# Two-way decayed scan with a sign-weight product on one core: transposes at the head of a step, sigmoids in threes, stores and halves moved

## The chip, the core and the metric

The kernel runs on 1 core of one Trainium2 chip. The metric is the device time of one execution in microseconds (us). Engines are named as the profile names them: PE (TensorE, the matrix engine), DVE (VectorE), ACT (ScalarE), POOL (GpSimd), SP (SyncE, which here only issues transfers).

## The reference

Inputs are x and k (4 x 1024 x 1024, float32), cond (4 x 256), w and u (1024), weight (1024 x 1024) and bias (1024). k stands for both k and v of the formula, x for r.

```
tf    = sigmoid(sum(cond))                         # one number a batch
decay = exp(-exp(w)) * (0.5 + 0.5 * tf)            # one a channel and batch
ek = exp(min(k, 30)); ekv = ek * k
nf, df = scan(a = a * decay + ekv), scan(b = b * decay + ek)   # along the sequence
nb, db = the same two scans backwards
euk = exp(min(u + k, 30))
num = nf + nb - ekv + euk * k
den = df + db - ek + euk
r   = sigmoid(x) * num / max(den, 1e-8) * (0.8 + 0.2 * tf)
out = x + r @ (sign(weight) * mean|weight|).T + bias
```

## The kernel before

**Tiles and steps.** The work is cut into N = 32 tiles, one for each batch (4) and each block of 128 channels (8). A tile is 128 channels x 1024 points of the sequence, with channels in partitions. `step(n)` of each engine runs once for each tile number n, and engines meet only through semaphores. The order in which an engine does its work is written out by hand in its block, and each engine does its list in that order. A tile goes through three steps: step n does its exponentials and scans, step n+1 its reciprocal and gate, step n+2 its numerator product and the split into two halves for the matrix product.

**What each engine does in step n**, with the names used below:

- DVE: `val` (L929) and `own` (L932) of tile n, both reading kT from PSUM; two scans forward (L901), two backward (L915); then **den** (L953), the denominator of tile n, the one full-size DVE operation of a step both of whose inputs lie in SBUF (euk and terms); then the **gate** of tile n-1 (L944), which multiplies the refined reciprocal in wkv by the turned sigmoid in sT. gate waits for POOL's inv of tile n-1 and for sT of tile n-1. val of tile n+1 follows.
- ACT: **Ln** and **Exp** of tile n-1 (L684, L686), the reciprocal by logarithm, which waits for den of tile n-1; from step 9 on a *clearing* (L663 takes a unit of the product out of PSUM to y_fm, L672 takes the turned unit before it to o_nat); **halves** of tile n-2 (L693, L695), after POOL's base; **two** of tile n-1 (L745), after POOL's chk; the three exponentials of tile n+1 (L649, L652, L653), which need kT; one or two more clearings; in steps 0 to 7 the preparation of a block of the weight (L774, L778, L795); and in some steps a **set** of sigmoids: table load, sigmoids in place on x_nat or x_end (L784, L790), table load back (L785, L791).
- POOL: **base** of tile n-2 (L363, after gate of tile n-2); **chk** of tile n-1 (L375, after Exp); **lo** of tile n-2 (L343, after halves); **inv** of tile n-1 (L381, after chk and two); an accumulating transfer of own (L384, after the third scan of DVE); and the **store** of a finished tile of the output (L356, an accumulating transfer from o_nat to DRAM, which waits until both halves are copied).
- PE: a unit is 16 matmuls of 128x512 (half a tile of the output over all 8 channel blocks). In step n: the first unit of the step, `s_turn(n-1)` (8 transposes of the sigmoid tile into sT), `k_turn(n+1)` (8 transposes of k into kT, after own of tile n), then the other units, each followed by the four transposes of the unit before (yT), which need ACT's clearing. From step 30 on PE makes the last batch's product, in the natural orientation (L484).
- SP: in step n the load of k of tile n+3 (after k_turn(n+1)), the load of x of tile n+2 (after s_turn(n-1), which frees the buffer), and copies of x into the output for the stores to add to.

`made(n)`, `cleared(n)` and `added` fix how many units are made and cleared by step n and in which step a tile is stored: two units a step in steps 9 to 18, two or three up to 24, three or more from 25. Tile m is stored in `summed(n)`: one a step in steps 11 to 27 and in 31, two in steps 28, 29 and 30. o_nat has four buffers, so the first copy of tile m waits until the store of tile m-4 has landed.

The sigmoid sets are made in even steps up to 24 (tiles n and n+1) and in steps 11, 13 and 15 (two each of the last six tiles, which lie in x_end).

Of the kernel before, what the change touches and what calls it, by code (L numbers as in the profile page):

```python
# [42 lines left out]
def bi_wkv_binary_ffn(nc, x, k, cond, w, u, weight, bias, out):  # L43
# [47 lines left out]
    with ExitStack() as ctx:  # L91
# [56 lines left out]
        two = sb("two", [P, 1])  # L148
# [104 lines left out]
        def _(sp):  # L253
# [28 lines left out]
            def step(n, p, wt, nxt, nxt3, mid, low, late):  # L282
                if wt:

                    done(sp, "sgn", n - 2)
                    done(sp, "abs", n - 2)
                    sp.dma_start(w_nat[p][:, :], weight.rearrange("(o p) i -> o p i", p=P)[n])\
                      .then_inc(w_in[p], 16)
                if n == 0:
                    load_x(2)  # L290
                if nxt3:

                    done(sp, "kT", n + 1)
                    sp.dma_start(k_nat[1 - p][:, :, :], tile_of(k, n + 3)).then_inc(k_in[1 - p], 16)
                if mid and n + 2 < SOON:

                    done(sp, "sT", n - 1)
                    load_x(n + 2)
                if 4 <= n < 10:
                    sp.dma_start(x_of(SOON + n - 4), tile_of(x, SOON + n - 4)).then_inc(s_soon, 16)  # L300
                if n == N - 2:

                    done(sp, "sT", N - 4)
                    load_tail(5)
                    done(sp, "kT", N - 2)
                    load_tail(6)
                if n == N - 1:

                    done(sp, "sT", N - 3)
                    load_tail(7)  # L310
                if 1 <= n <= 3 * TT:
                    fill((n - 1) // TT, (n - 1) % TT)
                if 1 <= n <= TT:
                    fill_last(n - 1)
# [18 lines left out]
        def _(pool):  # L333
# [31 lines left out]
            def step(n, p, wt, nxt, nxt3, mid, low, late):  # L365
                W, R = wkv[1 - p][:, :], rec[1 - p][:, :]
                if low:
                    base(n - 2)
                if 3 <= n < TT + 3:
                    biases(n - 3)  # L370
# [16 lines left out]
                for m in summed(n):  # L387
                    store(m)
# [23 lines left out]
        def _(pe):  # L412
# [90 lines left out]
            def step(n, p, wt, nxt, nxt3, mid, low, late):  # L503
# [30 lines left out]
                split = units[0:3 if n == LAST + 1 else 2] if first else ()  # L534
                if first and n != LAST + 1:
# [4 lines left out]
                if mid and not sooner:  # L540
                    s_turn(n - 1)
# [4 lines left out]
                if nxt:  # L546
                    k_turn(n + 1, 1 - p)
                if ahead:
# [82 lines left out]
        def _(act):  # L631
# [70 lines left out]
            act.wait_ge(s_const, 5)  # L702
# [12 lines left out]
            def step(n, p, wt, nxt, nxt3, mid, low, late):  # L715
# [6 lines left out]
                if n == N - 1:  # L722
                    early_out(4)
                    early_out(5)
                sooner = cleared(n - 1) if n == LAST + 2 else min(made(n - 1), cleared(n - 1) + 1)
# [10 lines left out]
                if late and n < N - 2:  # L736
                    clear(cleared(n - 1), sooner)
                if low:
# [3 lines left out]
                if mid:  # L742

                    done(act, "chk", n - 1)
                    act.activation(wkv[1 - p][:, :], wkv[1 - p][:, :], ACT.Identity,  # L745
                                   scale=-HI_SCALE * LO_GAIN, bias=two[:, 0:1]).then_inc(st["two"], 1)
# [33 lines left out]
                if p == 0 and n < SOON:  # L780

                    for i in range(2):
                        x_landed(act, n + i)
                        act.activation(x_of(n + i), x_of(n + i), ACT.Sigmoid).then_inc(st["sig"], 1)  # L784
                    act.preload_act_table_set("natural_log_exp_and_others")  # L785
                if n in (11, 13, 15):

                    for i in range(n - 11, n - 9):
                        act.wait_ge(s_soon, 16 * (N - SOON))
                        act.activation(x_of(SOON + i), x_of(SOON + i), ACT.Sigmoid).then_inc(st["soon"], 1)  # L790
# [49 lines left out]
        def _(dve):  # L840
# [15 lines left out]
            dve.memset(two[:, :], 2.0 * HI_SCALE * LO_GAIN).then_inc(s_const, 1)  # L856
# [197 lines left out]
```

## Time and profile before

| | |
|---|---|
| median of 3 runs (lowest, highest) | 529.12 us (527.07, 530.0) |
| the profiled execution: time, span | 530.84 us, 528.9 us |
| mean granted PE clock | 0.866 of full |
| busy, share of the span | PE 67%, DVE 93%, ACT 82%, POOL 72% |
| steps 1 to 30, start of den(0) to start of den(30) | 20.8 us to 471.2 us |
| from start of den(30) to the end of the span | 57.7 us |

The profiled execution's time is 1.9 us more than its span and 1.7 us above the median. In step n the stretch from one den to the next is what one tile costs. Below, den(n) is den of tile n, made in step n, and so for the others.

### The profile page before, as it was taken

How to read it: one execution, taken by the hardware profiler on the slowest of the kernel's cores; microseconds unless marked ns; L12 is line 12 of the kernel's file. 1: busy time of each engine (PE TensorE's matmuls, PEld its weight loads, DVE VectorE, ACT ScalarE, POOL GpSimd, SP SyncE). 2: the span in 40 equal slices, each digit the busy share in tenths (PEclk: the TensorE clock that was granted, in tenths of full speed). 3: DMA queues.
4: the chain of work that ended last, by engine and by line, in shares of the span. 5: the costliest groups of instructions: out<-in, count | busy, mean ns of one | idle time of the engine just before them, and what ended most of it. 6: DMA issues, size and time to landing. Idle time of an engine off the chain costs nothing.

```text
span 528.9 us, 5414 instructions
## 1 busy us (share of the span) xinstructions
PE 353.6 (67%) x1803; PEld 203.9 (39%) x1803; DVE 494.5 (93%) x347; ACT 431.8 (82%) x473; POOL 381.9 (72%) x210
## 2 busy tenths in 40 slices
PE   3332132333298775876768698878759995989996
PEld 2221122233054333443434354544425553544442
DVE  6999999999999999999999999899999999598676
ACT  3979899899989999999999979899698884884500
POOL 0058677858786877777788876969688776979483
PEclk9996565566698989898899998996979997999999
DMA  8677899999988778986879779597656569678469
GB/s 228 170 239 238 257 230 267 255 287 243 271 215 198 171 176 172 198 175 105 192 170 215 171 151 216 82 253 143 135 105 119 93 107 119 140 128 118 54 99 221
DMA packets 101283, 94.22 MB, mean 178 GB/s; under 512 B 2924, under 2 KB 93064, under 8 KB 100744
## 3 DMA queue, kind: packets, MB, share of 16 engines
q0 software_dynamic: 31440, 36.18, 45.1%
q1 hardware_dynamic: 67720, 56.65, 34.3%
q10 hardware_dynamic: 2096, 1.05, 0.7%
q8 instruction: 15, 0.25, 0.2%
q14 instruction: 12, 0.10, 0.1%
HBM read 60.31 MB, written 37.75 MB: 185 GB/s over the span
## 4 chain that ended last, share of the span: by engine, by line
ACT 42%; PE 26%; issue 12%; POOL 10%; DMA 5%; DVE 4%; SPq 0%; ACTq 0%; DVEq 0%; POOLq 0%
PE prod L443 11%; DMA out_dram<-o_nat 5%; ACT euk L653 5%; ACT rec L684 4%; POOL wkv L375 4%; POOL acts L343 4%; ACT x_nat L784 4%; ACT terms L649 3%; ACT y_fm L663 3%; PE prod L484 3%; ACT L785 3%; ACT L784 3%; ACT acts L693 2%; ACT o_nat L672 2%; ACT rec L695 2%
## 5 line engine op out<-in xcount | busy, mean ns | idle before, releaser
L443 PE MATMUL prod<-acts,sgn 128*128 128x512 f16 x752 | 189.2, 409 | 13.3 <-ACT orow L800 10.9
L915 DVE TENSOR_TENSOR_SCAN terms<-cols,y_start,terms 128x1024 f32<-128x1024 f32 x64 | 147.0, 2337 | 1.3 <-DVE y_start L907 0.2
L901 DVE TENSOR_TENSOR_SCAN terms<-cols,terms 128x1024 f32<-128x1024 f32 x64 | 142.7, 2269 | 0.0
L375 POOL TENSOR_TENSOR wkv<-euk,rec 128x1024 f32<-128x1024 f32 x31 | 76.3, 2462 | 62.2 <-ACT rec L686 62.2
L443 PEld LDWEIGHTS prod<-acts,sgn 128*128 128x128 f16 x752 | 78.1, 104 | 106.4 <-issue 24.9
L363 POOL TENSOR_TENSOR wkv<-wkv,terms 128x1024 f32<-128x1024 f32 x31 | 81.3, 2623 | 25.0 <-DVE wkv L944 24.9
L343 POOL TENSOR_TENSOR acts<-wkv,rec 128x1024 f16<-128x1024 f32 x30 | 71.2, 2375 | 22.5 <-ACT rec L695 22.5
L381 POOL TENSOR_TENSOR wkv<-wkv,rec 128x1024 f32<-128x1024 f32 x31 | 74.3, 2396 | 1.3 <-ACT wkv L745 1.3
L418 PE MATMUL yT<-ident,y_fm 128*128 128x128 f32 x192 | 31.5, 289 | 55.6 <-ACT o_nat L672 55.1
L953 DVE SCALAR_TENSOR_TENSOR euk<-euk,terms 128x1024 f32<-128x1024 f32 x31 | 63.8, 2058 | 1.1
L418 PE MATMUL prod<-ident,o_nat 128*128 128x128 f16 x64 | 8.3, 310 | 72.7 <-ACT o_nat L778 72.7
L418 PEld LDWEIGHTS yT<-ident,y_fm 128*128 128x128 f32 x192 | 22.7, 147 | 68.5 <-ACT y_fm L663 58.5
L944 DVE SCALAR_TENSOR_TENSOR wkv<-wkv,sT 128x1024 f32<-128x1024 f32 x31 | 37.5, 1211 | 8.7 <-POOL wkv L381 8.7
L356 POOL DMA_DIRECT2D out_dram<-o_nat x24 | 44.5, 1980 | 0.0
L649 ACT ACTIVATE terms<-kT,cap 128x1024 f32<-128x1024 f32 x31 | 34.2, 1102 | 11.4 <-PE kT L418 11.4
L418 PE MATMUL kT<-ident,k_nat 128*128 128x128 f32 x248 | 38.8, 309 | 6.4 <-DVE own L932 6.3
L663 ACT ACTIVATE y_fm<-prod,bcol,oscale 128x512 f32<-128x512 f32 x47 | 36.2, 771 | 6.7 <-PE prod L443 4.5
L672 ACT COPY o_nat<-yT 128x512 f32<-128x512 f32 x48 | 27.8, 580 | 16.7 <-DMA out_dram<-o_nat 11.4
L745 ACT ACTIVATE wkv<-wkv,two 128x1024 f32<-128x1024 f32 x31 | 35.3, 1140 | 7.3 <-POOL wkv L375 7.3
L384 POOL DMA_DIRECT2D terms<-own x32 | 28.8, 901 | 17.1 <-DVE terms L915 17.1
L929 DVE TENSOR_TENSOR terms<-terms,kT 128x1024 f32<-128x1024 f32 x32 | 38.7, 1211 | 2.2 <-ACT euk L653 2.2
L418 PE MATMUL sT<-ident,x_nat 128*128 128x128 f32 x208 | 35.2, 325 | 8.2 <-ACT x_nat L784 7.3
(122 smaller groups left out, 606.9 us busy)
## 6 DMA issues: line engine op xcount, KB each, us to landing
terms<-own POOLq DMA_DIRECT2D x32, 512.0 KB, 5.3
out_dram<-in_x_dram SPq DMA_DIRECT2D x32, 512.0 KB, 6.5
k_nat<-in_fside_BxSxS_dram SPq DMA_DIRECT2D x30, 512.0 KB, 3.9
x_nat<-in_x_dram SPq DMA_DIRECT2D x26, 512.0 KB, 5.9
out_dram<-o_nat POOLq DMA_DIRECT2D x24, 512.0 KB, 8.1
y_fm<-in_L_ffn_weight_dram SPq DMA_DIRECT2D x8, 512.0 KB, 7.3
out_dram<-in_L_ffn_bias_dram POOLq DMA_DIRECT2D x8, 512.0 KB, 6.7
x_end<-in_x_dram SPq DMA_DIRECT2D x6, 512.0 KB, 8.8
```

The lines of the kernel that those rows point to most:

```text
L343: pool.tensor_tensor(acts[:, 1, n % (2 * CT), :], wkv[p][:, :], rec[p][:, :], ALU.subtract)\
L356: pool.dma_start(tile_of(out, m), o_nat[m % NO][:, :, :], accum_op=ALU.add)\
L363: pool.tensor_tensor(wkv[n % 2][:, :], wkv[n % 2][:, :], ekv[n % NV], ALU.mult).then_inc(st["base"], 1)
L375: pool.tensor_tensor(W, euk[1 - p][:, :], R, ALU.mult).then_inc(st["chk"], 1)
L381: pool.tensor_tensor(W, W, R, ALU.mult).then_inc(st["inv"], 1)
L418: ins = pe.transpose(dst(q), what(q), one)
L443: ins = pe.matmul(made_in(u), view[:, c, m % CT * P:m % CT * P + P], acts[:, part, m // CT % 2 * CT + c, h * H:(h + 1) * H], start=(part = ...
L649: act.activation(ek[p], kT[:, :], ACT.Relu, scale=-1.0, bias=cap[:, 0:1]).then_inc(st["below"], 1)
L663: act.activation(y_fm[m % 2][:, h * H:(h + 1) * H], made_in(u), ACT.Identity, scale=oscale[:, m:m + 1], bias=bcol[:, m:m + 1]).then_inc(st ...
L901: dve.tensor_tensor_scan(buf, d, buf, 0.0, ALU.mult, ALU.add).then_inc(st["F" + kind], 1)
L915: dve.tensor_tensor_scan(buf[:, ::-1], d, buf[:, ::-1], y_start[:, i:i + 1], ALU.mult, ALU.add)\
L953: dve.scalar_tensor_tensor(U, U, E30, E, ALU.min, ALU.add).then_inc(st["den"], 1)
```

## The change

Six edits, all of order but the last two:

- **PE** in steps up to 25: s_turn and k_turn stand at the head of a step, ahead of its first unit. In steps 26 to 29 s_turn stood there already and k_turn stays behind the first unit.
- **SP**: the load of x stands ahead of the load of k.
- **ACT, sigmoids**: sets are made in steps 0, 3, 6, ... 24, each of tiles n, n+1 and n+2 (n+2 is loaded in the same step); from step 9 on each takes one tile of the last six with it. So there are 9 sets in place of 16, with 32 sigmoids as before. From step 9 to 21 a set has four sigmoids, before two.
- **ACT, halves**: in steps 4, 7, 10, ... 22 (those behind a set; a clearing stands there only from step 10 on) halves and two stand ahead of the first clearing, which comes behind two.
- **POOL**: the first store of a step stands behind base and ahead of chk, except in step 31; before, it stood at the end of the step. The second store of steps 28 to 30 stays at the end.
- **ACT, two**: the operation is Copy with a constant bias, before Identity with a bias from a tile; the tile `two` and its memset on DVE are gone, and a semaphore count goes from 5 to 4.

```diff
@@ SP, step
+                if mid and n + 2 < SOON:
+                    done(sp, "sT", n - 1)
+                    load_x(n + 2)
                 if nxt3:
                     done(sp, "kT", n + 1)
                     sp.dma_start(k_nat[1 - p][:, :, :], tile_of(k, n + 3)).then_inc(k_in[1 - p], 16)
-                if mid and n + 2 < SOON:
-                    done(sp, "sT", n - 1)
-                    load_x(n + 2)
@@ POOL, step
+                ready = summed(n)
                 if low:
                     base(n - 2)
+                if n < N - 1:
+                    for m in ready[0:1]:
+                        store(m)
+                    ready = ready[1:]
...
-                for m in summed(n):
+                for m in ready:
                     store(m)
@@ PE, step
+                if mid and not sooner:
+                    s_turn(n - 1)
+                    k_turn(n + 1, 1 - p)
+                if n == 0:
+                    k_turn(n + 1, 1 - p)
                 if first and n != LAST + 1:
                     done(pe, "ev", units[0] - 2)
                     part(units[0], 0, CT - 1)
                 elif units and not first:
                     unit(units[0])
-                if mid and not sooner:
-                    s_turn(n - 1)
+                if sooner:
+                    k_turn(n + 1, 1 - p)
                 if ahead:
                     turned(made(n) - 1)
                     for u in (made(n) + 1, made(n) + 2):
                         part(u, 0, CT - 2)
-                if nxt:
-                    k_turn(n + 1, 1 - p)
-                if ahead:
@@ ACT, step
+                hasty = low and n < LAST and n % 3 == 1
+                if hasty:
+                    done(act, "base", n - 2)
+                    halves(n - 2, p)
...
-                if late and n < N - 2:
+                if late and n < N - 2 and not hasty:
                     clear(cleared(n - 1), sooner)
-                if low:
+                if low and not hasty:
                     done(act, "base", n - 2)
                     halves(n - 2, p)
                 if mid:
                     done(act, "chk", n - 1)
-                    act.activation(wkv[1 - p][:, :], wkv[1 - p][:, :], ACT.Identity,
-                                   scale=-HI_SCALE * LO_GAIN, bias=two[:, 0:1]).then_inc(st["two"], 1)
+                    act.activation(wkv[1 - p][:, :], wkv[1 - p][:, :], ACT.Copy,
+                                   scale=-HI_SCALE * LO_GAIN, bias=2.0 * HI_SCALE * LO_GAIN).then_inc(st["two"], 1)
+                if late and hasty:
+                    clear(cleared(n - 1), sooner)
...
-                if p == 0 and n < SOON:
-                    for i in range(2):
-                        x_landed(act, n + i)
-                        act.activation(x_of(n + i), x_of(n + i), ACT.Sigmoid).then_inc(st["sig"], 1)
-                    act.preload_act_table_set("natural_log_exp_and_others")
-                if n in (11, 13, 15):
-                    for i in range(n - 11, n - 9):
+                if n % 3 == 0 and n < SOON:
+                    for i in range(n, min(n + 3, SOON)):
+                        x_landed(act, i)
+                        act.activation(x_of(i), x_of(i), ACT.Sigmoid).then_inc(st["sig"], 1)
+                    if n >= 9:
                         act.wait_ge(s_soon, 16 * (N - SOON))
-                        act.activation(x_of(SOON + i), x_of(SOON + i), ACT.Sigmoid).then_inc(st["soon"], 1)
+                        i = SOON + n // 3 - 3
+                        act.activation(x_of(i), x_of(i), ACT.Sigmoid).then_inc(st["soon"], 1)
                     act.preload_act_table_set("natural_log_exp_and_others")
```

POOL, from inv of step 11 to base of step 12, before (the third row is the transfer of own, the fourth the store):

```order
L381 TENSOR_TENSOR wkv0<-wkv0,rec0 128x1024
L384 DMA terms<-own1 128x1024
L356 DMA out_0_dram<-o_nat0 128x8x128
L363 TENSOR_TENSOR wkv0<-wkv0,terms 128x1024
L375 TENSOR_TENSOR wkv1<-euk1,rec1 128x1024
```

POOL, from base to base of step 11 after the change:

```order
L362 TENSOR_TENSOR wkv1<-wkv1,terms 128x1024
L355 DMA out_0_dram<-o_nat0 128x8x128
L379 TENSOR_TENSOR wkv0<-euk0,rec0 128x1024
L342 TENSOR_TENSOR acts<-wkv1,rec1 128x1024
L385 TENSOR_TENSOR wkv0<-wkv0,rec0 128x1024
L388 DMA terms<-own1 128x1024
```

The store of the first output tile has gone from behind own's transfer to between base and chk.

ACT, from the end of step 12 to the exponentials of step 13, before (set of two, then Ln, Exp, clearing, halves, two):

```order
L784 ACT_TABLE_LOAD
L784 ACTIVATE x_nat2<-x_nat2 128x1024
L784 ACTIVATE x_nat0<-x_nat0 128x1024
L785 ACT_TABLE_LOAD
L684 ACTIVATE rec0<-euk0,lnb 128x1024
L686 ACTIVATE rec0<-rec0 128x1024
L663 ACTIVATE y_fm1<-prod,bcol,oscale 128x512
L672 COPY o_nat1<-yT 128x512
L693 ACTIVATE acts<-wkv1 128x1024
L695 ACTIVATE rec1<-acts 128x1024
L745 ACTIVATE wkv0<-wkv0,two 128x1024
L649 ACTIVATE terms<-kT,cap 128x1024
```

ACT behind a later set, from the end of step 15 into step 16, after the change:

```order
L796 ACT_TABLE_LOAD
L796 ACTIVATE x_nat0<-x_nat0 128x1024
L796 ACTIVATE x_nat1<-x_nat1 128x1024
L796 ACTIVATE x_nat2<-x_nat2 128x1024
L801 ACTIVATE x_end<-x_end 128x1024
L802 ACT_TABLE_LOAD
L690 ACTIVATE rec1<-euk1,lnb 128x1024
L692 ACTIVATE rec1<-rec1 128x1024
L699 ACTIVATE acts<-wkv0 128x1024
L701 ACTIVATE rec0<-acts 128x1024
L755 ACTIVATE wkv1<-wkv1 128x1024
L669 ACTIVATE y_fm0<-prod,bcol,oscale 128x512
```

The set has grown by two sigmoids, and the clearing (L663, now L669) has gone behind two (L745, now L755).

PE in one step of two units, before and then after the change (sT is s_turn, kT is k_turn, prod a unit, yT the turning of a cleared unit):

```order
L443 MATMUL prod<-acts,sgn 128x512 x16
L418 MATMUL sT<-ident,x_nat2 128x128 x8
L418 MATMUL kT<-ident,k_nat0 128x128 x8
L418 MATMUL yT<-ident,y_fm1 128x128 x4
L443 MATMUL prod<-acts,sgn 128x512 x16
L418 MATMUL yT<-ident,y_fm0 128x128 x4
```

```order
L422 MATMUL sT<-ident,x_nat2 128x128 x8
L422 MATMUL kT<-ident,k_nat0 128x128 x8
L447 MATMUL prod<-acts,sgn 128x512 x16
L422 MATMUL yT<-ident,y_fm1 128x128 x4
L447 MATMUL prod<-acts,sgn 128x512 x16
L422 MATMUL yT<-ident,y_fm0 128x128 x4
```

The two turns have passed the first unit.

## Rows read from the trace of the kernel before

**Rows 1.** Timeline of DVE: start, us, operation (den in three steps).

```profile
107.14 1.22 DVE L953 SCALAR_TENSOR_TENSOR euk<-euk,terms 128x1024 f32<-128x1024 f32 x1
...
224.46 2.80 DVE L953 SCALAR_TENSOR_TENSOR euk<-euk,terms 128x1024 f32<-128x1024 f32 x1
...
239.96 2.79 DVE L953 SCALAR_TENSOR_TENSOR euk<-euk,terms 128x1024 f32<-128x1024 f32 x1
```

**Rows 2.** den alone (L953) by stage: length, busy us (times), PE clock, DMA, GB/s.

```profile
20.00:167.00 147.00, 19.88 (x11) 0.69 0.92 244
167.00:275.00 108.00, 18.65 (x7) 0.93 0.78 167
275.00:377.50 102.50, 11.54 (x7) 0.92 0.81 166
377.50:474.00 96.50, 13.74 (x6) 0.91 0.69 122
```

**Rows 3.** Timeline of POOL, in brackets idle before: step 15, then later steps.

```profile
228.48 2.52 POOL L363 TENSOR_TENSOR wkv<-wkv,terms 128x1024 f32<-128x1024 f32 x1
...
236.99 2.37 POOL L343 TENSOR_TENSOR acts<-wkv,rec 128x1024 f16<-128x1024 f32 x1 [0.83 <-ACT rec L695]
239.31 2.36 POOL L381 TENSOR_TENSOR wkv<-wkv,rec 128x1024 f32<-128x1024 f32 x1
...
242.19 1.92 POOL L356 DMA_DIRECT2D out_dram<-o_nat  x1
...
329.67 3.33 POOL L381 TENSOR_TENSOR wkv<-wkv,rec 128x1024 f32<-128x1024 f32 x1
...
437.27 3.52 POOL L356 DMA_DIRECT2D out_dram<-o_nat  x2
...
489.78 1.59 POOL L356 DMA_DIRECT2D out_dram<-o_nat  x1
```

**Rows 4.** DVE's waits, all of the span: total us, times, longest us.

```profile
DVE wkv L944 <- POOL wkv L381: 8.7, 3, 4.6
...
DVE terms L929 <- ACT euk L653: 2.2, 2, 2.0
```

**Rows 5.** Timeline of ACT: step 15 and the set behind it.

```profile
231.49 1.15 ACT L684 ACTIVATE rec<-euk,lnb 128x1024 f32<-128x1024 f32 x1
...
236.82 1.14 ACT L745 ACTIVATE wkv<-wkv,two 128x1024 f32<-128x1024 f32 x1
...
242.64 1.28 ACT L790 ACT_TABLE_LOAD   x1
243.93 2.00 ACT L790 ACTIVATE x_end<-x_end 128x1024 f32<-128x1024 f32 x2
...
247.25 1.15 ACT L684 ACTIVATE rec<-euk,lnb 128x1024 f32<-128x1024 f32 x1
```

**Rows 6.** Timeline of ACT: Ln in steps 2, 3 and 4.

```profile
37.45 1.14 ACT L684 ACTIVATE rec<-euk,lnb 128x1024 f32<-128x1024 f32 x1
...
54.16 1.14 ACT L684 ACTIVATE rec<-euk,lnb 128x1024 f32<-128x1024 f32 x1
...
67.37 1.14 ACT L684 ACTIVATE rec<-euk,lnb 128x1024 f32<-128x1024 f32 x1
```

**Rows 7.** Timeline of ACT in steps 24, 25 and 28: waits for kT and for a store.

```profile
374.82 1.11 ACT L649 ACTIVATE terms<-kT,cap 128x1024 f32<-128x1024 f32 x1 [4.04 <-PE kT L418]
...
382.80 1.15 ACT L684 ACTIVATE rec<-euk,lnb 128x1024 f32<-128x1024 f32 x1
...
445.54 0.59 ACT L672 COPY o_nat<-yT 128x512 f32<-128x512 f32 x1 [7.46 <-DMA out_dram<-o_nat]
```

**Rows 8.** PE behind that wait; then one stretch, busy us of PE, PEld, DVE, ACT, POOL.

```profile
446.26 1.08 PE L418 MATMUL yT<-ident,y_fm 128*128 128x128 f32 x4 [6.58 <-ACT o_nat L672]
...
448.85 5.28 PE L443 MATMUL prod<-acts,sgn 128*128 128x512 f16 x16
...
480.00:503.00 23.00, 23.00 (x112) 10.89 (x110) 16.80 (x19) 10.89 (x17) 15.03 (x10) 1.00 0.54 74
```

More of the change, by code:

```diff
@@ L147, in bi_wkv_binary_ffn @@
         lnb = sb("lnb", [P, 1])
-        two = sb("two", [P, 1])
         tiny = sb("tiny", [P, 1])
@@ L700, in early_out @@
                 act.copy(park[i], park_bank[i]).then_inc(st["early_sb"], 1)
-            act.wait_ge(s_const, 5)
+            act.wait_ge(s_const, 4)
             act.wait_ge(s_ucol, 2)
@@ L855, in _ @@
             dve.memset(lnb[:, :], LN_BIAS).then_inc(s_const, 1)
-            dve.memset(two[:, :], 2.0 * HI_SCALE * LO_GAIN).then_inc(s_const, 1)
             dve.memset(tiny[:, :], TINY).then_inc(s_const, 1)
```

## The prediction

> **What bounds the kernel now.** I read the busy shares first: DVE is busy for 93% of the span, and from step 1 to step 30 almost without a gap. But den is not the same length each time. It takes 1.22 us in one step and 2.80 in another, with the same shape [rows 1]. By stages its 31 runs sum to 19.88, 18.65, 11.54 and 13.74 us [rows 2]; less 1.22 for each that is 6.5, 10.1, 3.0 and 6.4 us, 26.0 in all, that den spends standing. The timelines of DVE and POOL laid side by side say for what. den(15) starts at 239.96 while inv runs from 239.31 to 241.67, and ends at 242.75, one den later than inv [rows 1, 3]. So a step has a wait inside a busy instruction: den, with both inputs in SBUF, stands while POOL computes. It goes the other way too: an inv that came while den ran, at 329.67, took 3.33 in place of 2.36 [rows 3], and gate waited for it instead. gate needs inv in any case, so the measure is how much later inv ends than den could start. Real idle time adds 4.6 (gate, step 29), 2.2 (gate, step 21), and 2.2 at val, mostly in step 29 [rows 4]; the last 1.9 of gate's 8.7 lie behind den(30). The four stages thus lose 6.5, 10.1, 5.5 and 13.0 us, 35.1 in all, against steps of 13.92 us. That is the step without loss: den to den 15.50 less (2.80 - 1.22) [rows 1].
>
> **The ring that makes inv late.** Let Z be the end of den(n-1), here 227.26. den(n) can start at Z + 12.70 (239.96). Ln starts at Z + 4.23, since ACT is still in a set, and inv ends at 241.67, that is 10.18 after Ln; 0.83 of it is POOL waiting for halves, which stand behind a clearing [rows 3, 5]. With halves ahead it is 9.35. So Ln may start up to Z + 2.5, or Z + 3.3 with halves ahead, and each us beyond costs one. In steps 10 to 16 ACT makes a set in every step, and it goes without a gap from Ln to Ln in 15.76 (231.49 to 247.25), so ACT sets the pace there, not DVE.
>
> **Sets by three.** A set of two costs 4.61 (242.64 to 247.25), of which the sigmoids are 2.00 and the two table loads with their ends 2.6 [rows 5]. Sixteen sets become nine: 7 x 2.6 = 18 us less on ACT, of which only what makes inv early counts. The other side is that a set of four takes 4.61 + 2.0 = 6.6 at a stretch.
>
> A price to weigh here: the first sigmoid stands 1.29 behind the start of the table load (242.64 to 243.93 [rows 5]), so a load brings no pause with it. The Trainium skill (ScalarE: Activation LUTs, What ACT_TABLE_LOAD costs) gives about 2.66 us a switch, a drain of 1.38 included. By the page a set of two would be 7.3 us and the cut 37 us; the row disagrees, and I go by the row.
>
> **Stores ahead of chk.** This lengthens POOL's own chain in every step that stores, 11 to 30. base starts at Z + 1.22 and POOL goes from one operation to the next in 2.32 (236.99 to 239.31). A store costs POOL 1.59 right behind an operation and 1.92 behind a transfer [rows 3]. So chk starts at Z + 5.1 to 5.4, not at Z + 3.5, and inv ends at best at Z + 12.1 to 12.4. That is inside 12.70, with 0.3 to 0.6 to spare: cost nothing on DVE. But two then starts at Z + 7.5 to 7.8, and ACT has 5.8 left behind it (236.82 to 242.64 [rows 5]): it ends at Z + 13.3 to 13.6, in time for the next Ln. In a set step it ends at Z + 20.1, so Ln starts at Z' + 6.0 to 6.2 (Z' = Z + 13.92), and inv ends 2.7 late, with halves ahead. The two steps that follow carry nothing over. The cost is 2.7 in three steps where it was about 1.6 in each.
>
> **The sum by stage.**
> - Up to den(10): no stores. ACT takes 13.2 for a step without a set (54.16 to 67.37) and 16.7 with one of two (37.45 to 54.16) [rows 6], so 17.7 with three: 44.1 for three steps against 41.8 of DVE. Worked forward from 38.5 in step 2, Ln of step 4 stands at 69.4, 6.5 behind den(3), which costs 3.1; that of step 7 costs 2.4; steps 2 and 10 some 0.2 each. 5.9 for 6.5.
> - 11 to 17: 2 x 2.7 = 5.4 for 10.1.
> - 18 to 24: step 19 costs 2.7; step 20, where the third unit is late as now, 0.3; step 22 follows a set with one more clearing behind it (1.1 more), 3.8. kT at the head takes away the wait of 4.04 in step 24 [rows 7] and with it the 0.3 at val. 6.8 for 5.5.
> - 25 to 30: without the wait of 4.04 for kT, Ln of step 25 starts 2 us earlier against DVE, though its set has three: from Z + 5.8 (382.80) to Z + 3.7, leaving 0.4 for 2.0. The store of tile 17 is issued at Z + 3.6 of step 28, near 426, not at 437.27; with 8.2 to land it is there at 434, before the copy that now waits 7.46 until 445.54 [rows 3, 7]. So the idle 4.6 and 2.0 and the long dens of 28 to 30 go. Three units a step still leave waits for PE: 0.5 to 1 a step. 3.0 for 13.0.
>
> 21.1 for 35.1: 14.0 us less. The profiled execution took 530.84, which gives 516.8; it stands 1.7 above the median, so 515.0.
>
> **What lies beside other work.** The turns at the head: PE waits for own of tile n until Z + 3.5 with a unit behind it, which before ran in that time. A unit is then made by Z + 8.1, and its clearing stands behind expU at Z + 12: hidden while there are two units. If that cover goes (three units, or a unit that takes 5.28 as at 448.85 [rows 8]), the last unit slips into the next step, up to 1 us a step. k's load behind x's: both wait for turns that are now earlier. The x tile of the same step is issued near Z + 2.5 and wanted, as third sigmoid, near Z + 16. With the 8.2 that the store of 437.27 took to land, the nearest row, it is there at Z + 10.7. two as Copy and a memset less: a few hundredths of a us on ACT, nothing on the path.
>
> **Does the tail keep it?** From 480 to 503 PE is busy for all of 23.00 us, DVE for 16.80 [rows 8], so the end is PE's. PE gains too: it was idle for 6.58 ahead of 446.26, and the 16 matmuls behind took 5.28, where 112 in 23.00 us make 3.3 for 16 [rows 8], 2.0 more. Together 8.6, and its last batch starts with lo(23), 2 us earlier against DVE. That is about what DVE gains in the last stage (10.0), so I take off nothing.
>
> **Rivals.**
> - *The late gain is not kept.* PE or the clearings behind it bound steps 26 to 31 in their own right, and PE's new idle time is spent again at the end. Then about half of the 10.0 is left: 518 to 523, say 520. For it: PE is full from 480. Against: its two stretches above. 16%.
> - *Sets cost little.* If ACT loses no time to chk in a set step, its load is what counts: 15.76 less 4.61 is 11.15 a step, with a set of four 40.1 in three steps, under the 41.8 of DVE. Then the 21.1 that is left shrinks to about 11, and the time is 505. Against: POOL's order holds two back until chk is through. 13%.
> - *POOL's chain is too long (slower).* The slack is 0.3 to 0.6 us. Two stores in a row took 3.52, 1.8 each [rows 3]. If a store between two operations holds POOL for 3.0, chk starts at Z + 6.5, inv ends at Z + 13.5 and each of 20 steps pays 0.8: 16 us, which takes the gain: 531. At 3.5 it is 541. It decides from about 2.9 us a store. Against: 1.59 in the one row of a store behind an operation. 8%.
> - *It does not do what it says:* x tiles of a set arrive late since their buffer comes free only in the same step. The margin is 5 us; if loads took 15, each of 8 sets would wait 1 to 2: 525. 4%.
>
> **Numbers.** Forecast 515.0 (510 to 520), 59%. With 16% for 518 to 523, 13% for about 505, 12% for 525 and more, the range is 505 to 524. One measurement of this kernel can tell about 0.5%, 2.6 us, from no change. Faster by more than that (below 526.5) 83%; within it 8%; slower 9%.
>
> **What would show it.** Right: den at 1.22 in all steps but those with n = 1 mod 3, where it is 3 to 4 or gate idles; two at Z + 7.5 behind a store; Ln right behind den in steps 12, 14, 15, 17; no wait of ACT for a store in steps 28 and 29; 19 table loads; PE full from about 465. Wrong: den long in every step with a store (third rival); ACT waiting for x or PE for sigmoids; den(30) early but the end not.

## The result, and the profile after

The changed kernel takes 514.12 us, median of four runs (513.96 to 514.45); the kernel before, beside it, 528.79 (527.07 to 530.0). The ratio is 0.9726, with a 95% interval of 0.9697 to 0.9754. The profiled execution took 513.96, with a span of 512.1 at a mean granted clock of 0.862. In what follows one run, of e8, took 757.95 us and stays out of that kernel's time and ratio.

The first lines of the page of after: span, busy shares, and the groups that answer to den, two, the store and gate (busy us, mean ns | idle us before, releaser).

```profile
span 512.1 us, 5399 instructions
...
PE 354.7 (69%) x1803; PEld 209.6 (41%) x1803; DVE 482.4 (94%) x346; ACT 411.1 (80%) x459; POOL 381.1 (74%) x210
...
L963 DVE SCALAR_TENSOR_TENSOR euk<-euk,terms 128x1024 f32<-128x1024 f32 x31 | 52.8, 1704 | 1.1
L755 ACT ACTIVATE wkv<-wkv 128x1024 f32<-128x1024 f32 x31 | 32.7, 1055 | 23.6 <-POOL wkv L379 23.6
...
L954 DVE SCALAR_TENSOR_TENSOR wkv<-wkv,sT 128x1024 f32<-128x1024 f32 x31 | 37.6, 1212 | 4.6 <-POOL wkv L385 4.6
...
L355 POOL DMA_DIRECT2D out_dram<-o_nat x24 | 39.9, 1662 | 0.0
```

DVE is the bound as before, and den still stands: 52.8 us in 31 runs, where 31 x 1.22 would be 37.8. By [rows 2] it was 63.8. A store holds POOL for 1.66 on average. den by stage, the same four stages as [rows 2]; columns length, busy us (times), PE clock, DMA share, GB/s:

```profile
20.00:177.00 157.00, 17.78 (x11) 0.70 0.92 242
177.00:278.00 101.00, 12.71 (x7) 0.92 0.85 178
278.00:381.00 103.00, 14.09 (x7) 0.90 0.76 165
381.00:460.00 79.00, 8.24 (x6) 0.96 0.81 136
```

Less 1.22 for each run this is 4.4, 4.2, 5.6 and 0.9 us (before 6.5, 10.1, 3.0 and 6.4). With the idle time of DVE in each step added (gate 4.6 in all, in steps 4 and 22; before 8.7) I get what each stage loses against 13.92 us a step. The same count, made step by step up to the end of den(30), for every kernel of this study (the prediction had before at 35.1 by its own count; waits behind den(30) are not in it, and two counts of the same stage can differ by 0.2):

| kernel | to den(10) | 11 to 17 | 18 to 24 | 25 to 30 | sum |
|---|---|---|---|---|---|
| before | 6.6 | 10.2 | 5.7 | 13.1 | 35.6 |
| forecast for after | 5.9 | 5.4 | 6.8 | 3.0 | 21.1 |
| after | 6.9 | 4.2 | 7.9 | 0.9 | 19.9 |
| e1: stores alone | 6.6 | 10.1 | 5.1 | 0.0 | 21.9 |
| e2: after, stores at the end | 7.2 | 1.9 | 5.8 | 8.9 | 23.8 |
| e3: after, stores ahead only late | 7.0 | 1.8 | 5.7 | 1.5 | 16.1 |
| e4: after, clearing first | 8.5 | 6.0 | 8.0 | 1.6 | 24.1 |
| e5: after, PE as before | 6.4 | 4.2 | 7.0 | 3.4 | 21.0 |
| e6: sets alone | 7.7 | 2.9 | 4.1 | 13.1 | 27.9 |
| e7: after, den with PSUM operand | 4.9 | 2.2 | 3.8 | 2.9 | 13.9 |
| e8: e3, clearing first in step 19 | 7.9 | 1.7 | 4.0 | 1.3 | 14.8 |
| e9: after, bias transfer last | 7.4 | 4.2 | 7.0 | 1.4 | 20.1 |
| e10: e3, bias transfer last | 7.8 | 1.6 | 3.7 | 1.4 | 14.5 |

**A step with a set and the step behind it.** DVE first: Z is the end of the den at 179.45, so 180.67; den(12) starts at 193.37, den(13) at 207.29.

```profile
179.45 1.23 DVE L963 SCALAR_TENSOR_TENSOR euk<-euk,terms 128x1024 f32<-128x1024 f32 x1
...
193.37 1.23 DVE L963 SCALAR_TENSOR_TENSOR euk<-euk,terms 128x1024 f32<-128x1024 f32 x1
...
207.29 3.28 DVE L963 SCALAR_TENSOR_TENSOR euk<-euk,terms 128x1024 f32<-128x1024 f32 x1
```

POOL in the same two steps: the store between base (L362) and chk (L379), then lo (L342) and inv (L385).

```profile
181.90 2.36 POOL L362 TENSOR_TENSOR wkv<-wkv,terms 128x1024 f32<-128x1024 f32 x1 [2.13 <-DVE wkv L954]
184.22 1.59 POOL L355 DMA_DIRECT2D out_dram<-o_nat  x1
185.19 2.99 POOL L379 TENSOR_TENSOR wkv<-euk,rec 128x1024 f32<-128x1024 f32 x1
187.51 3.00 POOL L342 TENSOR_TENSOR acts<-wkv,rec 128x1024 f16<-128x1024 f32 x1
189.83 2.98 POOL L385 TENSOR_TENSOR wkv<-wkv,rec 128x1024 f32<-128x1024 f32 x1
...
202.51 2.35 POOL L379 TENSOR_TENSOR wkv<-euk,rec 128x1024 f32<-128x1024 f32 x1 [2.78 <-ACT rec L692]
...
207.14 2.34 POOL L385 TENSOR_TENSOR wkv<-wkv,rec 128x1024 f32<-128x1024 f32 x1
```

ACT: Ln (L690), two (L755), then the set of four and the next Ln.

```profile
180.71 1.15 ACT L690 ACTIVATE rec<-euk,lnb 128x1024 f32<-128x1024 f32 x1 [0.95 <-DVE euk L963]
...
188.22 1.06 ACT L755 ACTIVATE wkv<-wkv 128x1024 f32<-128x1024 f32 x1 [1.78 <-POOL wkv L379]
...
193.68 1.28 ACT L796 ACT_TABLE_LOAD   x1
194.97 2.95 ACT L796 ACTIVATE x_nat<-x_nat 128x1024 f32<-128x1024 f32 x3
197.83 1.04 ACT L801 ACTIVATE x_end<-x_end 128x1024 f32<-128x1024 f32 x1
198.89 1.28 ACT L802 ACT_TABLE_LOAD   x1
200.19 1.15 ACT L690 ACTIVATE rec<-euk,lnb 128x1024 f32<-128x1024 f32 x1
```

Step 12 shows the slack of the prediction: inv ends at 192.81, Z + 12.1, and den, which can start at Z + 12.7, is 1.23 long. In step 13 Ln starts at 200.19, 5.6 behind den(12); inv runs from 207.14 to 209.48, den comes at 207.29 into it and stands: 3.28.

**The late steps.** Here [rows 7] had a wait of 7.46 for a store. In after ACT has no wait for a store at all, and losses are 0.0 in steps 28 to 30. From 463 to 486 PE has no gap (length; PE, PEld, DVE, ACT, POOL; clock, DMA share, GB/s), as [rows 8] had from 480:

```profile
463.00:486.00 23.00, 23.00 (x113) 10.94 (x111) 17.33 (x20) 10.26 (x16) 15.06 (x10) 1.00 0.36 52
```

### The profile page after: what moved, and what is told of

It reads as the page before. It is cut to its first block, busy times and chain, and to the rows that moved or that the text cites. A ratio compares the mean times of both kernels' runs of the same rounds, so it can differ in the third digit from the quotient of the medians.

```text
span 512.1 us, 5399 instructions
## 1 busy us (share of the span) xinstructions
PE 354.7 (69%) x1803; PEld 209.6 (41%) x1803; DVE 482.4 (94%) x346; ACT 411.1 (80%) x459; POOL 381.1 (74%) x210
## 3 DMA queue, kind: packets, MB, share of 16 engines
q1 hardware_dynamic: 67720, 56.65, 35.1%
q10 hardware_dynamic: 2096, 1.05, 0.8%
## 4 chain that ended last, share of the span: by engine, by line
POOL 23%; ACT 23%; PE 22%; issue 16%; DVE 14%; DMA 0%; SPq 0%; DVEq 0%; ACTq 0%; POOLq 0%
POOL wkv L379 9%; PE prod L447 8%; DVE terms L925 4%; POOL acts L342 4%; DVE terms L911 4%; POOL wkv L385 4%; POOL out_dram L355 3%; PE prod L488 3%; ACT x_nat L796 3%; ACT rec L690 2%; ACT terms L655 2%; ACT euk L659 2%; ACT rec L692 2%; PE sT L488 2%; PE kT L488 2%
## 5 line engine op out<-in xcount | busy, mean ns | idle before, releaser
L447 PE MATMUL prod<-acts,sgn 128*128 128x512 f16 x752 | 180.2, 395 | 0.0
L362 POOL TENSOR_TENSOR wkv<-wkv,terms 128x1024 f32<-128x1024 f32 x31 | 73.4, 2367 | 50.7 <-DVE wkv L954 50.7
L379 POOL TENSOR_TENSOR wkv<-euk,rec 128x1024 f32<-128x1024 f32 x31 | 82.3, 2654 | 37.2 <-ACT rec L692 37.2
L385 POOL TENSOR_TENSOR wkv<-wkv,rec 128x1024 f32<-128x1024 f32 x31 | 81.8, 2639 | 1.2 <-ACT wkv L755 1.2
L342 POOL TENSOR_TENSOR acts<-wkv,rec 128x1024 f16<-128x1024 f32 x30 | 77.7, 2590 | 4.7 <-ACT rec L701 4.6
L422 PE MATMUL kT<-ident,k_nat 128*128 128x128 f32 x248 | 45.9, 347 | 16.7 <-DVE own L942 16.5
L963 DVE SCALAR_TENSOR_TENSOR euk<-euk,terms 128x1024 f32<-128x1024 f32 x31 | 52.8, 1704 | 1.1
L755 ACT ACTIVATE wkv<-wkv 128x1024 f32<-128x1024 f32 x31 | 32.7, 1055 | 23.6 <-POOL wkv L379 23.6
L388 POOL DMA_DIRECT2D terms<-own x32 | 35.8, 1120 | 17.4 <-DVE terms L925 17.2
L422 PEld LDWEIGHTS kT<-ident,k_nat 128*128 128x128 f32 x248 | 38.7, 184 | 23.7 <-issue 22.7
L422 PEld LDWEIGHTS sT<-ident,x_nat 128*128 128x128 f32 x208 | 31.3, 179 | 28.8 <-issue 16.3
L669 ACT ACTIVATE y_fm<-prod,bcol,oscale 128x512 f32<-128x512 f32 x47 | 36.1, 769 | 4.8 <-PE prod L447 2.7
L422 PEld LDWEIGHTS yT<-ident,y_fm 128*128 128x128 f32 x192 | 23.8, 148 | 38.9 <-ACT y_fm L669 32.7
L690 ACT ACTIVATE rec<-euk,lnb 128x1024 f32<-128x1024 f32 x31 | 35.7, 1151 | 4.5 <-DVE euk L963 4.4
```

Of the source, the lines that this page charges most:

```text
L342: pool.tensor_tensor(acts[:, 1, n % (2 * CT), :], wkv[p][:, :], rec[p][:, :], ALU.subtract)\
L362: pool.tensor_tensor(wkv[n % 2][:, :], wkv[n % 2][:, :], ekv[n % NV], ALU.mult).then_inc(st["base"], 1)
L379: pool.tensor_tensor(W, euk[1 - p][:, :], R, ALU.mult).then_inc(st["chk"], 1)
L385: pool.tensor_tensor(W, W, R, ALU.mult).then_inc(st["inv"], 1)
L422: ins = pe.transpose(dst(q), what(q), one)
L447: ins = pe.matmul(made_in(u), view[:, c, m % CT * P:m % CT * P + P], acts[:, part, m // CT % 2 * CT + c, h * H:(h + 1) * H], start=(part = ...
```

## The experiments

Times are medians; ratios are to the kernel before, run on the same chip, with 95% intervals. The load of x ahead of the load of k, and two as a Copy (1.06 us in place of 1.14), were not tried alone.

**e1, stores alone.** Before, with the first store of a step behind base:

```diff
+                ready = summed(n)
                 if low:
                     base(n - 2)
+                if n < N - 1:
+                    for m in ready[0:1]:
+                        store(m)
+                    ready = ready[1:]
...
-                for m in summed(n):
+                for m in ready:
```

> The kernel before with one edit: the first store of a step ahead of chk. Theory (near the end the store frees o_nat in time; elsewhere it costs only where rec comes before Z + 5): in steps 12 to 17 rec comes at Z + 6.5 and nothing changes; the losses of steps 28 to 30 (1.8, 6.7 and 1.5 us) and nearly 1 us of the tail go; behind the sets of steps 18 to 24 some 3 us are added: about 520.5 us. Rival (the late gain of the change comes from PE's new order): the waits for a store go but the end stays, 526 to 529 us.

518.43 us, 0.9786 (0.9754 to 0.9818), so 11.3 less. The last stage goes from 13.1 to 0.0, though PE's order is that of before. Steps 27 to 30 had 11.1 of it, and there the store frees o_nat in time. The other 2.0, in step 25, went in another way: ACT's wait for kT in step 24 fell from 4.04 to 0.15 (by all steps from 11.4 to 7.8), and PE ran at another clock. PE in step 24, before and then e1:

```profile
364.27 1.94 PE L418 MATMUL sT<-ident,x_nat 128*128 128x128 f32 x8 [0.90 <-DVE wkv L944]
366.85 7.05 PE L443 MATMUL prod<-acts,sgn 128*128 128x512 f16 x24
```

```profile
363.92 1.06 PE L423 MATMUL sT<-ident,x_nat 128*128 128x128 f32 x8 [0.90 <-DVE wkv L949]
365.26 5.34 PE L448 MATMUL prod<-acts,sgn 128*128 128x512 f16 x24
```

From 364 to 370 the granted clock was 0.50 in before and 1.00 in e1. No run shows that the store did this, so these 2.0 us are not shown to be the stores'. Steps 18 to 24 change little: 0.6 less at step 20, 0.9 less at 21, 1.1 more at 19. The time is 2 us below the 520.5 expected. Steps 10 to 17 are unchanged to 0.1: a store ahead of chk costs nothing there even with a set in every step. That speaks against the third rival, which wanted 0.8 a step.

**e6, sets alone.** Before, with the set block of after:

```diff
-                if p == 0 and n < SOON:
+                if n % 3 == 0 and n < SOON:
...
-                    for i in range(2):
+                    for i in range(n, min(n + 3, SOON)):
...
-                if n in (11, 13, 15):
+                    if n >= 9:
```

> The kernel before with one edit: sigmoids in sets of three (from step 9 four). Theory (in steps 11 to 17 ACT sets the pace, 15.5 us a step, and is freed): the loss of 10.1 us there falls to about 4, up to step 10 it grows by 1, from 18 to 24 it stays, near the end it stays: about 522.5 us. Rival (the sets alone change only when ACT waits, and the gain needs halves ahead of the clearing): 527 us or more.

524.23 us, 0.9896 (0.9856 to 0.9931), 5.5 less. Steps 11 to 17 lose 2.9 in place of 10.2, the last stage its 13.1 as before. This is 1.7 above the 522.5 expected. e1 and e6 together would give 16.8; after, with further edits, gives 14.5: stores and sets get in each other's way, and e3 shows where.

**e2, stores back at the end of the step**, else as after:

```diff
-                if n < N - 1:
-                    for m in ready[0:1]:
-                        store(m)
-                    ready = ready[1:]
```

> The changed kernel with every store back at the end of its step. Theory (a store ahead of chk costs 1.6 us on POOL, holds two back to Z + 7.5 and so lengthens what is left of a set step, but frees o_nat in time near the end): behind sets two no longer waits, the loss in steps 13, 16 and 19 falls from 2.05 us to about 1.0 and in step 22 from 3.2 to about 2.2, together 4 us less; the waits of ACT for a store in steps 28 to 30 come back, 8 to 9 us more. Sum 514.1 + 4.5 = about 518.5 us. Rival (the loss behind a set does not depend on the store): 2.05 stays in steps 13, 16, 19, and the time is about 522.5 us.

519.36 us, 0.9827 (0.9784 to 0.9869), near the 518.5 expected. The last stage loses 8.9 (after 0.9), gate stands idle for 2.25 more behind den(30), and the wait of [rows 7] is back in the timeline of ACT (in brackets the idle time ahead of the copy into o_nat):

```profile
436.17 0.58 ACT L674 COPY o_nat<-yT 128x512 f32<-128x512 f32 x1 [7.50 <-DMA out_dram<-o_nat]
```

But steps 11 to 17 lose only 1.9, and 18 to 24 only 5.8. Stores at the head pay late and cost early.

**e3, stores at the head only from step 25 on:**

```diff
-                if n < N - 1:
+                if LAST < n < N - 1:
```

> The changed kernel with stores at the head only in steps 25 to 30, at the end up to step 24. Theory: takes both gains, losses behind sets of 1.0 in steps 13, 16, 19 and about 2.2 in step 22, no wait for a store near the end: 514.1 - 4 = about 510 us, faster than the changed kernel. Rival: the store's place up to step 24 has no weight, 514 us.

509.17 us, 0.9638 (0.9598 to 0.9679): faster than both kernels, as expected, and 4.7 less than after by the ratios, whose intervals don't meet. From e2 it differs only in the stores from step 25 on, and these are worth 10.2 us. Step 12 and 13 of POOL: inv and own's transfer first, then the store; and den(13) behind it.

```profile
188.92 2.36 POOL L385 TENSOR_TENSOR wkv<-wkv,rec 128x1024 f32<-128x1024 f32 x1
191.47 0.90 POOL L388 DMA_DIRECT2D terms<-own  x1 [0.19 <-issue]
192.07 1.92 POOL L355 DMA_DIRECT2D out_dram<-o_nat  x1
```

```profile
207.36 2.53 DVE L963 SCALAR_TENSOR_TENSOR euk<-euk,terms 128x1024 f32<-128x1024 f32 x1
```

den(13) stands for 1.3 in place of 2.06, den(16) for 0.5 in place of 2.08, and step 22 loses 1.8 in place of 3.2. In a set step ACT's list waits for two, two for chk, and chk for the store; in the steps without a set, ACT has time to spare.

**e4, the clearing ahead of halves in every step:**

```diff
-                hasty = low and n < LAST and n % 3 == 1
+                hasty = False
```

> The changed kernel with the first clearing ahead of halves in every step, as before the change. Theory (lo waits for halves, so inv ends 0.8 us later behind each set): losses in steps 10, 13, 16, 19 and 22 grow by 0.8 each, the others stay: about 518 us. Rival (ACT's debt behind a set is what counts, and the place of the clearing within the step is free): 514 us, and lo starts right behind chk in these steps all the same.

518.06 us, 0.9814 (0.9775 to 0.9853), 4.7 more than after: the time expected, but by other terms. Steps 10, 13, 16, 19 and 22 lose 1.7, 0.9, 0.9, 0.9 and 0.9 more. But step 20 goes from 1.64 to 0.0, more than halves ahead bring in step 19. In after, the clearing behind two in step 19 comes late, the third unit with it. ACT up to the halves of step 20:

```profile
300.75 0.78 ACT L669 ACTIVATE y_fm<-prod,bcol,oscale 128x512 f32<-128x512 f32 x1 [1.60 <-issue]
...
304.64 0.78 ACT L669 ACTIVATE y_fm<-prod,bcol,oscale 128x512 f32<-128x512 f32 x1 [0.50 <-PE prod L447]
...
305.78 1.07 ACT L699 ACTIVATE acts<-wkv 128x1024 f16<-128x1024 f32 x1
```

ACT stands 1.6 ahead of the last clearing of step 19 and 0.5 ahead of the first of step 20; halves follow at 305.78, and lo on POOL, which waits 1.42 for them, makes inv late. The 1.6 end when PE's unit does. It took 5.30, at a mean granted clock of 0.68, behind 3.10 us in which PE waited for the late clearing. In e10 (below), which has the same order here, PE stood for 1.41 and the unit took 3.62, at full clock. PE in step 19, after and then e10:

```profile
294.89 0.63 PE L422 MATMUL yT<-ident,y_fm 128*128 128x128 f32 x4 [3.10 <-ACT o_nat L678]
295.36 5.30 PE L447 MATMUL prod<-acts,sgn 128*128 128x512 f16 x16
```

```profile
291.65 0.63 PE L422 MATMUL yT<-ident,y_fm 128*128 128x128 f32 x4 [1.41 <-ACT o_nat L678]
292.11 3.62 PE L447 MATMUL prod<-acts,sgn 128*128 128x512 f16 x16
```

Step 20 lost 1.64 in after and 0.45 in e10.

**e8, e3 with the clearing ahead of halves in step 19 alone:**

```diff
-                hasty = low and n < LAST and n % 3 == 1
+                hasty = low and n < LAST and n % 3 == 1 and n != 19
```

> The changed kernel with stores at the head only in steps 25 to 30, and in step 19 the clearing ahead of halves again. Theory (in step 19, the first with three units, a clearing behind two delays PE's third unit into step 20): step 19 loses 0.9 us more, step 20 loses 1.6 less, so 0.7 us less than with stores at the head only in steps 25 to 30, about 508.5 us. Rival (step 20 loses for another reason): 510 us.

508.76 us, 0.9622 (0.9581 to 0.9662). Step 20 loses 0.0, and step 19 the same 1.35, not 0.9 more as expected. So the place of the clearing is shown as a cause of step 20's loss; how much it costs hangs on PE's clock behind it, as e10 shows with 0.45. The time can't be told from e3's: step 10 lost 0.9 more, step 13 0.8 less and step 16 0.7 more, where nothing was changed. Step 9 on PE explains the first of these. In after: sT and kT turns, then the two units of the step.

```profile
138.58 1.94 PE L422 MATMUL sT<-ident,x_nat 128*128 128x128 f32 x8 [8.25 <-DVE wkv L954]
140.84 1.65 PE L422 MATMUL kT<-ident,k_nat 128*128 128x128 f32 x8 [0.32 <-DVE own L942]
142.33 7.07 PE L447 MATMUL prod<-acts,sgn 128*128 128x512 f16 x32
```

And in e8:

```profile
138.58 1.94 PE L422 MATMUL sT<-ident,x_nat 128*128 128x128 f32 x8 [8.24 <-DVE wkv L954]
140.84 1.94 PE L422 MATMUL kT<-ident,k_nat 128*128 128x128 f32 x8 [0.32 <-DVE own L942]
142.57 7.90 PE L447 MATMUL prod<-acts,sgn 128*128 128x512 f16 x32
```

PE idles 8.25 ahead of the turns, and from 136 to 142 the granted clock is 0.50 (1.2 GHz). From 142 to 150 it is 1.00 in after, 0.86 in e8: the same 32 matmuls take 7.07 and 7.90. The clearing of step 9 and the set of four behind it start 1.1 later, and step 10 loses 2.7 in place of 1.6, most of it with gate idle.

**e9, the bias transfer of steps 3 to 10 behind own's transfer,** not between base and chk, else as after:

```diff
-                if 3 <= n < TT + 3:
-                    biases(n - 3)
...
                 pool.dma_start(ekv[n % NV], own[p][:, :], accum_op=ALU.add).then_inc(num_in[p], 16)
+                if 3 <= n < TT + 3:
+                    biases(n - 3)
```

> The changed kernel with the transfer of the bias (steps 3 to 10) issued behind own's transfer at the end of POOL's step, not between base and chk. It asks where the 1.62 us that den(10) loses in the changed kernel comes from. There chk of step 9 starts 2.89 behind base, where 2.32 is usual, and two waits 1.05 for it, ahead of a set of four. Theory (POOL's chain in step 9): two of step 9 comes 0.58 earlier, the set and Ln of step 10 with it, less what the clearings then wait for PE (they wait 0.37 now, 0.9 then at most): the loss of step 10 goes from 1.62 to 1.05 to 1.3, all other steps as they are, time 513.7 (513 to 514.5). Rival (the clearings wait for the unit of PE in any case, so the set starts no earlier): step 10 stays at 1.6, time 514.1. The time can't tell them apart; the set's start behind den(8) in the timeline does.

515.32 us, 0.9736 (0.9703 to 0.9769), above the 513 to 514.5 expected and not to be told from after. two of step 9 comes earlier, at 142.96 in place of 144.12 (0.3 of it because all of DVE stands 0.3 earlier here), but step 10 loses 2.33. ACT in step 9:

```profile
142.96 1.06 ACT L755 ACTIVATE wkv<-wkv 128x1024 f32<-128x1024 f32 x1 [0.17 <-POOL wkv L377]
...
149.44 0.78 ACT L669 ACTIVATE y_fm<-prod,bcol,oscale 128x512 f32<-128x512 f32 x1 [1.90 <-PE prod L447]
```

What POOL gave, ACT waits for PE: the rival's mechanism holds, though not its 1.6 for step 10. With the turns at the head the two units of this step start only at 142.3, and here they took 7.47, at a granted clock of 0.93 from 142 to 150. So the set starts at 150.24, later than in after (149.86), and with den(8) 0.3 earlier.

**e10, both:** e3 with that move.

> The changed kernel with stores at the head only from step 25 on, and the bias transfer behind own's transfer. Expected as the kernel with late stores alone (509.2), less 0.3 to 0.6 for step 10: 508.8. It is the fastest list of edits so far, if step 10 gives anything; rival: step 10 unchanged and 509.2.

508.53 us, 0.9609 (0.9572 to 0.9646), within the interval of e3; step 10 lost 2.7, as in e8, at a granted clock of 0.87 from 142 to 150, so no gain from the move is shown. In both kernels step 13 then lost only 0.5: steps 10 and 13 together lost 3.15 in each, and 3.06 in e3.

**e5, PE's order of before,** else as after:

```diff
-                if mid and not sooner:
-                    s_turn(n - 1)
-                    k_turn(n + 1, 1 - p)
...
                     unit(units[0])
+                if mid and not sooner:
+                    s_turn(n - 1)
+                if nxt:
+                    k_turn(n + 1, 1 - p)
```

> The changed kernel with PE's order of before (unit, s_turn, k_turn, then the others), all else as changed. Theory (the turns at the head matter in step 24, where kT comes 4 us sooner, and cost where there are three units): step 25 loses about 2 us more, steps 20 and 24 up to 2 us less, x tiles of a set land in time: 514 to 516 us. Rival (the sets by three need the turns at the head, since the buffer of the third tile comes free only behind s_turn): ACT waits for x in steps 12 to 21, 1 to 3 us each: 519 us or more.

516.44 us, 0.9753 (0.9725 to 0.9781), 1.4 more than after by the ratios and not quite told apart; ACT waits for no x tile, so the rival is out. In the trace step 10 loses 0.5 less, step 24 0.9 less, steps 25 and 27 1.4 and 1.0 more, and step 20 the same: 1.1 in sum. Step 24 is the place where the head order hurts. In after PE turns yT of the unit before only behind kT, and both at the low clock (0.50 from 362 to 365); ACT waits for it:

```profile
362.32 1.94 PE L422 MATMUL kT<-ident,k_nat 128*128 128x128 f32 x8 [0.73 <-DVE own L942]
364.06 1.06 PE L422 MATMUL yT<-ident,y_fm 128*128 128x128 f32 x4
```

```profile
365.15 0.59 ACT L678 COPY o_nat<-yT 128x512 f32<-128x512 f32 x1 [3.69 <-PE yT L422]
```

**e7, den with one input in PSUM.** It asks whether den's length is standing:

```diff
+                    if mid:
+                        done(dve, "sT", n - 1)
-                    dve.scalar_tensor_tensor(U, U, E30, E, ALU.min, ALU.add)
+                    dve.scalar_tensor_tensor(U, U, E30, sT[:, :] if mid else E, ALU.min, ALU.add)
```

> The changed kernel in which den takes its second operand from sT in PSUM and not from ek in SBUF (in steps 1 to 30): the same size, the sums of the denominator are left out. Theory (den stands while POOL reads SBUF, and gate then comes one den later than inv ends): den takes 1.22 us in every step, gate waits idle for inv instead, and each of the steps 4, 7, 10, 13, 16, 19, 20, 22 and 24 loses about 1.0 us less: about 505.5 us. Rival (den is long for a reason of its own, or the wait for inv sets all of the loss): den stays long, or the loss stays the same with gate idle for all of it: 514 us.

509.02 us, 0.9636 (0.96 to 0.9673), 4.8 less than after. The kernel leaves the sums of the denominator out, so that only its time says something. den in this kernel (ns least, median, most), the den and gate of step 7, and the sum of DVE's waits for inv:

```profile
L965 DVE SCALAR_TENSOR_TENSOR euk<-euk,sT x30: 1220/1221/1223, 33.5 to 451.0; 128x1024 f32<-128x1024 f32 x30
```

```profile
118.89 1.22 DVE L965 SCALAR_TENSOR_TENSOR euk<-euk,sT 128x1024 f32<-128x1024 f32 x1
122.08 1.22 DVE L954 SCALAR_TENSOR_TENSOR wkv<-wkv,sT 128x1024 f32<-128x1024 f32 x1 [1.97 <-POOL wkv L385]
```

```profile
DVE wkv L954 <- POOL wkv L385: 11.1, 11, 2.2
```

All 30 are 1.22 long, also where POOL computes: the excess of [rows 1, 2] is standing, for its second input in SBUF. What remains is gate's open wait for inv, 11.1 us where after shows 4.6. In step 13 den's loss of 2.06 has become a wait of 1.03: a den that stands waits for inv's end and then takes its own 1.22 behind it, where one that doesn't stand runs beside inv. The time came out 3.5 above the 505.5 expected, for two reasons in the trace. Step 7 kept 2.05: from two of step 6 on ACT has no pause until Ln, which starts at 112.77 where after has 113.03. And steps 26 and 27 lose 1.17 and 1.46, where after loses 0.0 and 0.50. What holds these two I haven't settled. Step 20 lost 1.2 less, but that is not den's: PE stood for 1.61 in step 19 and its unit took 3.62, as in e10.

The Trainium skill (SBUF — State Buffer, Who interferes with whom) says that a DVE instruction with two SBUF inputs contends with a GpSimd instruction that reads SBUF, one with at most one SBUF input, outside the two-port modes, doesn't, and that the order of issue decides who blocks. The runs agree: up to 3.42 against 1.22 for den, and inv at 3.33 where it came second (before, at 329.67).

## Why the prediction was right

**Stores ahead of chk: right to 0.1 us.** Forecast in a step without a set: two at Z + 7.5 to 7.8, inv's end at Z + 12.1 to 12.4, den at Z + 12.70. Measured: 188.22, 192.81 and 193.37, so Z + 7.5, 12.1 and 12.7. In 11 to 17 only steps 13 and 16 lose anything, as said.

**The loss behind a set: right in kind, too large.** 2.7 was forecast, 2.06, 2.08 and 2.07 were measured (steps 13, 16, 19). Ln stands at Z' + 5.6, not 6.0 to 6.2: the set of four took 6.51 (193.68 to 200.19), and the list from two to the set 5.46, where [rows 5] had 5.82. Steps 4, 7 and 22 were 2.82, 2.20 and 3.24 for 3.1, 2.4 and 3.8. Over the six steps this is 2.9 less than forecast.

**Step 10: 1.62 for 0.2.** The working went by ACT's load alone. In step 9 of after, halves wait 1.34 and two 1.05 for POOL, and the sum had neither; no run takes these waits away alone. It also left out that with the turns at its head PE starts the first two units only at 142.3, behind own of step 9, and that the clearing ahead of the set needs them (e9). The turns are the smaller part: with PE's order of before (e5) the two waits for POOL are the same and step 10 still loses 1.13. Behind 8.25 us of idle PE the granted clock from 142 to 150 differed, and with it the loss: 1.6 at 1.00 (after), 2.7 at 0.86 (e8).

**Step 20: 1.64 for 0.3.** I took the third unit to be late "as now" and didn't follow the clearing of step 19, which had just moved behind two. e4 and e8, each with that clearing ahead, show 0.0. In e10 and e7, which have it behind as after has, the loss is 0.45 and 0.46: there PE idled less and its unit took 3.62, not 5.30. So about 1.2 of the 1.64 came with the lower granted clock, which the sum didn't reckon with.

**Step 24: 0.92 for 0.** The wait of [rows 7] for kT is gone, as forecast, and the one for yT took its place: 3.69 us for 4.04. The turn at the head passed one unit and one yT, and only the unit was counted.

**The last stage: 0.9 for 3.0.** The wait of 7.46 and the long dens of 28 to 30 went, as said. The 0.5 to 1 a step set aside for PE was too much: ACT waits for PE there 0.7 at most, and only steps 25 and 27 lose, 0.4 and 0.5. That kT at the head has a part in this gain, as I wrote, e5 bears out: without it ACT waits 1.74 for kT in step 24, step 25 loses 1.4 more and step 27 1.0. e1, which has 0.0 with PE's order of before, had PE at the full clock in step 24.

**The sum.** Terms too large by 2.9 + 2.1 and too small by 1.4 + 1.3 + 0.9 nearly cancel: 19.9 for 21.1. The start of den(30) moved from 471.2 to 456.8. Behind it the span shrank by 2.5 more, of which 1.5 is den(30) itself, counted in the sum; 1.0 is beyond it. The profiled executions differ by 16.9 us, where 14.0 were forecast; the medians by 14.7, as that of before stood 2.1 above the median of the runs beside the new kernel, and that of after 0.2 below its own. The forecast took off 1.7. The mechanism held where most of the gain was forecast, but that the median came within 0.9 of 515.0 is in part luck: terms of the sum that cancel, and a profiled run of before that stood higher above its median than was taken off.

**The rivals.** The late gain was kept, 12.2 of 13.1. "Sets cost little" did not hold in after; e3, with the store out of the set steps, brings the 19.9 down to 16.1, but its 509.2 is still 4 us above the rival's 505. "POOL's chain is too long" fell by the 1.59 of each store behind base and by e1. x tiles are never waited for by the set: their load lands in 3.6 us (median), margin kept.

## What to carry to other kernels

A piece of work that is moved costs only in those steps where the engine behind it has no time to spare, so ask for each step by itself: here the store at the head is worth 10 us from step 25 on (e2 against e3) and costs 5 in the fourteen steps before (after against e3). e3 takes the gain and leaves the cost. Where an instruction with two SBUF inputs is longer than its fellows, read its length as a wait and look at what POOL does then. When work is put at the head of a list, count everything that it passes (units and yT), not only the one it was meant to pass. And before a loss in one step is put down to an edit, compare the granted clock of that step in both traces.

## What the runs showed of the hardware that I had not expected

- Behind a store three POOL operations are recorded as 2.99, 3.00 and 2.98 us, but start 2.32 apart (185.19, 187.51, 189.83), as those of 2.35 do: the records overlap by 0.67, and the work isn't slower. Their ends can be trusted: chk's is at 188.18, and two, which waits for it, starts at 188.22. So it is the starts that are recorded early. From the end of base (184.26) to the end of chk is 3.92, so the store costs 1.60, its own recorded length. The Trainium skill (Perfetto Trace Analysis, GPSIMD Engine Instruction) calls the recorded span of such instructions unreliable and advises to time them from start to start. For the three operations the trace agrees; for the store it doesn't, as from base's start to chk's there are 3.29, only 0.97 more than 2.32.
- The granted clock of a stretch behind an idle one differs between executions of the same instructions: 1.00, 0.98 (e3) and 0.86 (e8) from 142 to 150, with all that is ahead of it alike. It moved the loss of step 10 by 0.9 to 1.1 us, between kernels that don't differ up to there. Between e3 and e8 step 13 gave nearly all of it back. How much of the spread between runs comes from it wasn't tried.
- Elsewhere, where the work ahead was not timed quite alike, the granted clock differed too: 24 matmuls of step 24 took 7.05 us in before and 5.34 in e1, and 16 of step 19 took 5.30 in after and 3.62 in e10. The loss of the step behind differed by 2.0 and 1.2 us.
